# Five put-off recurrences instead of four between two expert mixtures

## The reference, cut to what matters

```python
f, i, o = sigmoid(...)   # of gates = xn @ W.T + b
z = tanh(...)
c = f * c + i * z                       # along the 512 tokens
h = o * tanh(layer_norm(c, ln_w, ln_b))
```

## Time and profile before

| | us |
|---|---|
| median of 3 runs | 1192.91 (1192.29 to 1193.06) |
| the profiled execution: its own time | 1204.18 |
| its span, first to last instruction | 1201.7 |
| last unit of the first mixture done on PE | 949.89 |
| first matmul of the second mixture | 1009.98 |

### The profile page before, as it was taken

How to read it: one execution, slowest core, us unless ns; L and a number is a source line. 1 busy time by engine, 2 the same in 40 slices (tenths; PEclk the granted TensorE clock), 3 DMA queues, 4 the chain that set the end, 5 groups by cost and what they waited for, 6 DMA issues and landing times. The chain is left out here.

```text
span 1201.7 us, 18211 instructions
## 1 busy us (share of the span) xinstructions
PE 1008.9 (84%) x5032; PEld 418.2 (35%) x5032; DVE 870.2 (72%) x1795; ACT 768.9 (64%) x1460; POOL 609.1 (51%) x632
## 2 busy tenths in 40 slices
PE   4699999999898999778998989989999874888870
PEld 3123232333333322133443443434344332454440
DVE  4698889898989898845777676767676553555554
ACT  1066666667676777666776767767777533777751
POOL 5422323332332312356678869686878630355555
PEclk9999999999999999989999999999999976999995
DMA  2462825131331402789998989896879424122126
GB/s 62 75 133 64 200 73 107 38 58 41 53 66 27 75 11 60 185 221 206 223 170 209 184 200 186 195 220 161 216 157 192 101 103 148 46 65 75 59 79 241
DMA packets 118757, 149.72 MB, mean 125 GB/s; under 512 B 18217, under 2 KB 72089, under 8 KB 118223
## 3 DMA queue, kind: packets, MB, share of 16 engines
q1 hardware_dynamic: 111854, 139.65, 50.2%
q0 software_dynamic: 6272, 8.94, 2.4%
q10 hardware_dynamic: 544, 0.13, 0.2%
HBM read 109.44 MB, written 40.04 MB: 124 GB/s over the span
## 5 line engine op out<-in xcount | busy, mean ns | idle before, releaser
L762 ACT ACTIVATE a_probs<-a_score 128x512 f32<-128x512 f32 x512 | 293.1, 597 | 126.7 <-PE a_score L843 120.1
L940 DVE TENSOR_REDUCE a_mx<-a_mxps 128x2 f32<-128x1024 f32 x256 | 306.0, 1213 | 38.1 <-PE a_mxps L834 37.5
L1539 POOL TENSOR_TENSOR m_hidl<-m_hid,m_hidh 128x512 f16<-128x512 f32 x222 | 258.0, 1176 | 98.3 <-ACT m_hidh L1602 92.7
L1811 DVE TENSOR_TENSOR m_hid<-m_h,p_gates 128x512 f32<-128x512 f32 x215 | 146.3, 686 | 73.4 <-ACT m_h L1608 53.2
L1608 ACT ACTIVATE m_h<-m_h 128x512 f32<-128x512 f32 (+1 forms) x264 | 153.5, 582 | 36.6 <-PE m_h L1716 33.7
L1602 ACT ACTIVATE m_hidh<-m_hid 128x512 f16<-128x512 f32 x222 | 137.7, 620 | 53.6 <-DVE m_hid L1811 39.1
L855 PE MATMUL a_ops<-a_probs,a_vst 128*32 128x512 f32 x1024 | 136.4, 605 | 0.8 <-ACT a_probs L762 0.8
L1694 PE MATMUL m_y<-m_hidh,p_wdh 128*128 128x512 f16 (+1 forms) x264 | 100.6, 381 | 27.6 <-POOL m_hidl L1539 25.9
L2103 POOL DMA_INDIRECT t_picked<-e_yrow,p_rows x77 | 76.1, 988 | 89.5 <-DVE e_yrow L2236 67.4
L2247 DVE SCALAR_TENSOR_TENSOR e_hidl<-e_h,e_hidh 128x468 f16<-128x468 f32 (+1 forms) x96 | 57.9, 603 | 73.9 <-ACT e_hidh L2119 45.6
L843 PE MATMUL a_score<-a_qstack,a_kstack 128*128 128x512 f16 x256 | 96.9, 384 | 8.6 <-ACT a_probs L762 7.0
(11 more groups left out here) (263 smaller groups left out, 1882.9 us busy)
## 6 DMA issues: line engine op xcount, KB each, us to landing
p_gates<-t_cw SPq DMA_DIRECT2D x256, 256.0 KB
t_slots<-p_blank SPq DMA_DIRECT2D x8, 723.9 KB
p_rows<-t_slots SPq DMA_DIRECT2D x7, 723.9 KB
t_qparts<-a_qparts SPq DMA_DIRECT2D x32, 128.0 KB
t_picked<-p_blank SPq DMA_DIRECT2D x8, 512.0 KB
p_raw<-up SPq DMA_DIRECT2D x8, 512.0 KB, 5.5
p_raw<-down SPq DMA_DIRECT2D x8, 512.0 KB, 6.3
a_xin<-x SPq DMA_DIRECT2D x8, 256.0 KB, 3.7
```

What stands on the lines that cost most here:

```text
L762: act.activation(probs[:, kt % 2, g, :], score[:, g % 2, :], ACT.Exp, scale=SCALE / (QS * QS)).then_inc(exp_done, 1)
L940: dve.tensor_reduce(mx[ahead % 2][:, j // 2, g:g + 2], mxps[:, j % 2, :, :], AX.X, ALU.max).then_inc(mx_done, 1)
L1539: pool.tensor_tensor(hidl[0:r0, k % r, :], hid[0:r0, k % r, :], hidh[0:r0, k % r, :], ALU.subtract).then_inc(lo_done[0], 1)
L1811: dve.tensor_tensor(gated, h, gates[:, q % (SLOTS * GROUP), :], ALU.mult).then_inc(mul_done, 1)
```

## The change

- Recurrence 3 leaves stage 6 and becomes the first of five put off to the gap.
- `PE_END`, `ACT_END`, `DVE_END` and `END_BANK` are new, and `POOL_END` gives POOL's order: here all eight `send` come between the `crstd` of recurrence 3 and that of 4.
- Recurrences 6 and 7 get buffers of their own (`room`): the late buffers lie in `hid`, `hidh` and `hidl`, which the units no longer need there. So 6 and 7 no longer wait for 4 and 5. The statistics exist four times.
- Semaphores that two kinds of step shared (`c_rel`) are two now (`cn_rel`, `s1_rel`); `prod_done` and `x_added` become one.
- The wait for the landing of the recurrences' stores moves from the end of the mixture's block on SP to the start of the next block, ahead of `kept_rows`.

```diff
-RECUR_IN = {1: 0, 3: 1, 5: 2, 6: 3}
-PUT_OFF = (4, 5, 6, 7)
-XN_RING = len(PUT_OFF) + 1
-DVE_END = ((7, "prod"), (4, "lin_f"), (7, "xadd"), (7, "stats"), (4, "iz"), (4, "scan"), (7, "norm"), (4, "cstats"),
-           (4, "caggr"), (7, "top0"), (7, "top1"), (5, "lin_f"), (7, "share"), (7, "slots"), (4, "cnorm"), (5, "iz"),
-           (5, "scan"), (4, "s1"), (5, "cstats"), (5, "caggr"), (6, "lin_f"), (6, "iz"), (6, "scan"), (6, "cstats"),
-           (6, "caggr"), (5, "cnorm"), (7, "lin_f"), (7, "iz"), (7, "scan"), (5, "s1"), (7, "cstats"), (7, "caggr"),
-           (6, "cnorm"), (6, "s1"), (7, "cnorm"), (7, "s1"))
+RECUR_IN = {1: 0, 3: 1, 5: 2}
+PUT_OFF = (3, 4, 5, 6, 7)
+XN_RING = len(PUT_OFF)
+PE_END = ((3, "f"), (3, "i"), (7, "prodT"), (3, "z"), (3, "o"), (4, "f"), (4, "i"), (3, "cT"), (4, "z"), (7, "xnT"),
+    (4, "o"), (7, "logits"), (3, "nT"), (5, "f"), (5, "i"), (3, "sR"), (7, "rank"), (5, "z"), (4, "cT"), (5, "o"), (6,
+    "f"), (6, "i"), (6, "z"), (6, "o"), (5, "cT"), (7, "f"), (7, "i"), (7, "z"), (7, "o"), (6, "cT"), (7, "cT"), (4,
+    "nT"), (5, "nT"), (4, "sR"), (6, "nT"), (5, "sR"), (6, "sR"), (7, "nT"), (7, "sR"))
+DVE_END = ((7, "prod"), (3, "lin_f"), (7, "xadd"), (7, "stats"), (3, "iz"), (3, "scan"), (7, "norm"), (3, "cstats"),
+    (3, "caggr"), (4, "lin_f"), (4, "iz"), (3, "cnorm"), (7, "top0"), (7, "top1"), (3, "s1"), (7, "share"), (4,
+    "scan"), (7, "slots"), (4, "cstats"), (4, "caggr"), (5, "lin_f"), (5, "iz"), (5, "scan"), (6, "lin_f"), (5,
+    "cstats"), (5, "caggr"), (6, "iz"), (6, "scan"), (7, "lin_f"), (7, "iz"), (6, "cstats"), (6, "caggr"), (7,
+    "scan"), (4, "cnorm"), (5, "cnorm"), (4, "s1"), (6, "cnorm"), (5, "s1"), (7, "cstats"), (7, "caggr"), (6, "s1"),
+    (7, "cnorm"), (7, "s1"))
+POOL_END = ((7, "rstd"), (3, "crstd"), (7, "send"), (7, "send"), (7, "send"), (7, "send"), (7, "send"), (7, "send"),
+    (7, "send"), (7, "send"), (4, "crstd"), (5, "crstd"), (6, "crstd"), (7, "crstd"))
...
     def early(self):
-        return self.index() < 2
+        return self.index() < 2 or self.index() >= BATCH - 2
+    def room(self):
+        return self.p + 2 * (self.index() >= BATCH - 2)
...
-        gate_f, cell, s1 = ([sb(f"{n}{p}", [P, TOK]) for p in range(2)] for n in ("gate_f", "cell", "s1"))
-        cn = [sb(f"cn{p}", [P, TILES, D]) for p in range(2)]
+        gate_f = buffers("gate_f", [hid[:, 4, :], hid[:, 5, :]])
+        cell, s1, cn = (buffers(n, [wide_part(t, k) for t in (hidh, hidl)]) for k, n in enumerate(("cell", "s1", "cn")))
...
             for late in PUT_OFF[1:]:
                 store_s(stage_of(late))
-            for p in range(2):
-                sp.wait_ge(s_out[p], 16 * PASSES)
...
         @block.sync
         def _(sp):
+            for p in range(2):
+                sp.wait_ge(pre.s1_out[p], 16 * PASSES)
             kept_rows(sp, scratch, kept, kept_in)
```

More of the change, by code:

```diff
@@ L143, in __init__ @@
         self.gate_in = [sem(f"gate_in{k}") for k in range(SLOTS)]
+        self.s1_out = [sem(f"s1_out{p}") for p in range(2)]
         self.blank = sb("blank", [P, REC])
@@ L1185, in bank_plan @@
             continue
[L1186 removed]
+        if key[1] in ("prodT", "xnT"):
             use(key, turn % NBANKS)
@@ L1327, in mixture_phase, with buffers, wide_part @@
         prod = sb("prod", [P, TOK])
+        def buffers(name, late):
+            return [sb(f"{name}{p}", [P, TOK])[:] for p in range(2)] + late
+        def wide_part(t, k):
+            return t[:].rearrange("p r x -> p (r x)").bitcast(F32)[:, k * TOK:k * TOK + TOK]
         xnew = sb("xnew", [P, TILES, D])
@@ L1333, in mixture_phase @@
         stats, mv = sb("stats", [P, TILES, 6]), sb("mv", [P, TILES, 2])
-        cstats, cmv = ([sb(f"{n}{p}", [P, TILES, k]) for p in range(2)] for n, k in (("cstats", 6), ("cmv", 2)))
+        cstats, cmv = ([sb(f"{n}{p}", [P, TILES, k]) for p in range(4)] for n, k in (("cstats", 6), ("cmv", 2)))
         vareps, rstd = (sb(n, [P, TILES, 1]) for n in ("vareps", "rstd"))
-        cvareps, crstd = ([sb(f"{n}{p}", [P, TILES, 1]) for p in range(2)] for n in ("cvareps", "crstd"))
+        cvareps, crstd = ([sb(f"{n}{p}", [P, TILES, 1]) for p in range(4)] for n in ("cvareps", "crstd"))
         rec = [sb(f"rec{p}", [P, TILES, REC]) for p in range(2)]
@@ L1393, in mixture_phase @@
         c_moments, c_inverse = sem("c_moments"), sem("c_inverse")
-        bias_done, s_out = sem("bias_done"), [sem(f"s_out{p}") for p in range(2)]
+        bias_done, s_out = sem("bias_done"), pre.s1_out
         top, tgap_done, shared_out, counting = (sem(n) for n in ("top", "tgap", "shares", "counting"))
@@ L1430, in bank_free @@
             else:
-                eng.wait_ge(c_rel, old.n("c_rel", 1 + (use == "nT")))
+                eng.wait_ge(cn_rel if use == "cT" else s1_rel, old.n("once", 1))
         JOB_AT = {(0, 0, 0, 8): 0, (0, 0, 0, 16): 1, (0, 0, 0, 24): 2, (0, 0, 1, 12): 3, (0, 1, 0, 12): 4,
@@ L1582, in _ @@
                 further(LAST.back(), q)
[L1583 to L1590, removed]
+            places = iter(range(SENDS))
+            for b, name in POOL_END:
+                if name == "rstd":
+                    inverse_std(stage_of(b))
+                elif name == "crstd":
+                    inverse_cell_std(stage_of(b))
+                else:
+                    send(stage_of(b), next(places))
         @block.scalar
@@ L1648, in step @@
                             else:
-                                act.wait_ge(c_rel, b.twice("c_rel", 2))
-                        act.activation(tg[name][b.p][:], src, ACT.Tanh, scale=0.5, bias=bgh[:, w:w + 1]
+                                act.wait_ge(s1_rel, b.twice("once", 1))
+                        act.activation(tg[name][b.room()], src, ACT.Tanh, scale=0.5, bias=bgh[:, w:w + 1]
                                        ).then_inc(gate_done, 1)
@@ L1657, in step @@
                     act.wait_ge(sR_full, b.n("once", 1))
-                    if not b.early():
+                    if b.index() >= 2:
                         act.wait_ge(s_out[b.p], b.half("dma", 0))
@@ L1737, in step @@
                 if name == "prodT":
-                    pe.wait_ge(prod_done, b.n("once", 1))
+                    pe.wait_ge(prod_done, b.n("sums", 1))
                     for t in range(TILES):
@@ L1844, in step @@
                     dve.tensor_tensor(bank(b, "prodT"), xres[b.p][:].rearrange("p t d -> p (t d)"), bank(b, "prodT"),
-                                      ALU.add).then_inc(x_added, 1)
+                                      ALU.add).then_inc(prod_done, 1)
                 elif name == "stats":
-                    dve.wait_ge(x_added, b.n("once", 1))
+                    dve.wait_ge(prod_done, b.n("sums", 2))
                     if not b.first():
@@ L1869, in step @@
                     dve.wait_ge(gate_done, b.n("gates_full", 1))
-                    dve.tensor_scalar(gate_f[b.p][:], bank(b, "f"), 0.5, 0.5, ALU.mult, ALU.add).then_inc(cell_step, 1)
+                    dve.tensor_scalar(gate_f[b.room()], bank(b, "f"), 0.5, 0.5, ALU.mult, ALU.add).then_inc(cell_step, 1)
                 elif name == "iz":
@@ L1874, in step @@
                     dve.wait_ge(gate_done, b.n("gates_full", 3))
-                    dve.scalar_tensor_tensor(bank(b, "z"), tg["i"][b.p][:], 1.0, bank(b, "z"), ALU.add, ALU.mult
+                    dve.scalar_tensor_tensor(bank(b, "z"), tg["i"][b.room()], 1.0, bank(b, "z"), ALU.add, ALU.mult
                                              ).then_inc(cell_step, 1)
@@ L1881, in step @@
                         dve.wait_ge(sR_full, b.twice("once", 1))
-                    dve.scalar_tensor_tensor(s1[b.p][:], tg["o"][b.p][:], 1.0, bank(b, "nT"), ALU.add, ALU.mult
-                                             ).then_inc(c_rel, 1)
+                    dve.scalar_tensor_tensor(s1[b.room()], tg["o"][b.room()], 1.0, bank(b, "nT"), ALU.add, ALU.mult
+                                             ).then_inc(s1_rel, 1)
                 elif name == "scan":
@@ L1888, in step @@
                         dve.wait_ge(cT_full, b.twice("once", 1))
-                    dve.tensor_tensor_scan(cell[b.p][:], gate_f[b.p][:], bank(b, "z"), 0.0, ALU.mult, ALU.add
+                    dve.tensor_tensor_scan(cell[b.room()], gate_f[b.room()], bank(b, "z"), 0.0, ALU.mult, ALU.add
                                            ).then_inc(cell_step, 1)
@@ L1893, in step @@
                     dve.wait_ge(cT_full, b.n("once", 1))
-                    if not b.early():
-                        dve.wait_ge(c_inverse, b.twice("inverse", 2))
+                    if b.index() >= 4:
+                        dve.wait_ge(c_inverse, b.n("inverse", 2 - 4 * PER["inverse"][0]))
                     apart(dve)
                     for t in range(TILES):
-                        dve.bn_stats(cstats[b.p][:, t, :], bank(b, "cT")[:, t * P:t * P + P]).then_inc(c_moments, 1)
```

(1 more changed line is left out.)

52 lines of the change are left out of this document (25 added, 27 removed).

## The result

The changed kernel takes 1175.61 us (median of 4 runs, 1173.87 to 1180.63), the kernel before on the same chip 1192.99 (4 runs, 1192.29 to 1193.57): ratio 0.9861, 95% interval 0.9828 to 0.9895, so 17.4 us less. The profiled execution of after has a span of 1171.2 us and an own time of 1173.87.

The account below looks back on a forecast made before the run. PE was taken to bound stage 6, and a chain across engines, laid out along DVE, the gap. Stage 4.6, gap 10.8 and moved wait 1.8 sum to 17.2 us less: 1192.9 to 1175.7, range 1171 to 1183.

Parts of the forecast that it names:

- 12.6 was forecast: Gap before the second mixture: 10.8 us less from DVE's work and holes, 1.8 from the moved wait.
- Stage 6, 4.6 less: Stage 6 without recurrence 3 becomes like stage 7: 56.0 to 51.4 us, 4.6 less; bounds 3.6 and 6.1.
- DVE's work, 38.9: In the gap, DVE's steps with hops take 32.8 us plus 6.1 for one more recurrence: 38.9.
- Holes, 5.0 taken, 4.2 laid out: DVE's waits in the new gap, 21.9 us before: layout gives 4.2, 5 taken; bounds 3 and 7.6.
- POOL is half a microsecond ahead at `cnorm` 4: In the gap after the eight sends, `crstd` 4 is ready at 980.8 and DVE reaches `cnorm` 4 at 981.3.
- PE's clock: In the gap, clock near 1.00 up to the last `o` gate, PE sparse only afterwards, when DVE leads.
- The rival of half the clock in all of the gap: PE bounds the gap at half clock: 19 us of holes, 3.2 us gained in all, 1189.7; chance 0.07.
- The moved wait, 1.8: SP's wait for store landings leaves the mixture block's end for the next block: 1.8 us less, costing nothing there.
- What could be late next: Token-row loads done at 989, next phase at 997.4, so hidden; copies of 6 and 7 waiting for stores cost 1.8 at most.
- No hole of the old size: Rival: the new order holds as many DVE holes in the gap as the old; no change, 1192.6; chance 0.04.
- No send held for a step: Rival: each POOL send in the gap is held for one DVE step of 0.69 us: 5 us lost, 1180.7; chance 0.05.
- The rule on the port pair: GpSimd transfer descriptors can't be written while a vector step holds the shared ports; 0.13 us at most in the old trace.

Follow-up runs that it names:

- experiment 10: Changed kernel with 41 matmuls whose result nobody reads added in PE's list through the end of the gap; 1171.56 us, ratio 0.9829 to the kernel before, gap 44.82.
- experiment 9: Changed kernel with the gap's `lin_f` moved from DVE to ACT and the four lists reordered, `crstd` 4 between sends; 1171.61 us, ratio 0.984, gap 43.27.
- experiment 2: Changed kernel's code (buffers, semaphores, moved wait) with the old lists and recurrence 3 back in stage 6; 1191.67 us, ratio 0.9982 to the kernel before, gap 57.60.
- run 3: Changed kernel with recurrence 3 kept in stage 6, so four recurrences in the new lists; 1181.96 us, ratio 0.9912 to the kernel before, gap 48.11.
- run 6: Also experiment 6: changed kernel with two more scans on DVE behind `caggr` 4; 1189.32 us, ratio 0.9895 to the kernel before, gap 49.46.
- second group: Four kernels on another chip: four recurrences with loads first, 1193.24 us; changed kernel with wait put back, 1186.9; with two DVE scans, 1189.32; with one POOL operation, 1185.96.

## Why the prediction came out right

The sum, 17.2 us against 17.4 measured (1175.7 against 1175.6), is right in its terms as well, but that it fits to 0.2 us is luck: errors of up to 1.4 us go against each other, and two profiles of the kernel before differ by 1.8 us in the gap that it starts from. By the table the gap gained 13.9 us between the first profiles and 12.1 between the second ones, where 12.6 was forecast.

- *Stage 6, 4.6 less.* Measured 4.8 and 5.7. The stage has 50.3 to 51.2 us, about as stage 7 had (51.4); stage 7 is 0.2 to 0.8 longer now, which the sum had at nothing.
- *DVE's work, 38.9.* Measured 42.72 from first step to last less 5.2 of waits: 37.5. The term was 1.4 too large. It was worked out from steps with waits between them. Steps without a wait between them overlap in the timeline: `lin_f` of 3 has 0.69 us, and `xadd` starts 0.60 behind its start. From start to start, waits taken out, a recurrence's seven steps are 5.7 us on average in the new gap, 5.9 in the old and 6.1 in the sum.
- *Holes, 5.0 taken, 4.2 laid out.* Measured 5.2, and at the places named: 0.45 `lin_f` (0.4), 0.35 `share` (0.4), 0.36 `s1` 4 (0.6), 0.54 `cnorm` 7 (0.7), 2.12 the last `s1` (2.1). The second profile has none before `share`, 0.77 before `s1` 4 and the same in all (5.3). Not foreseen: 0.45 before `cnorm` 4, 0.41 before `cstats` 5, 0.29 before `cnorm` 3 and 0.25 before `s1` 6. The step that failed, though not by enough to show, is that POOL is half a microsecond ahead at `cnorm` 4: it is behind by 0.45. POOL is ready 30.8 us behind the last down matmul, as laid out (30.9), and DVE already at 30.4, 1.0 sooner than the 31.4 laid out.
- *PE's clock.* The forecast was "near 1.00 up to the last `o` gate". In one profile it was 0.83 in 955 to 965 and in the other 1.00, with the same gap of 46.2; behind the last gate it is low for the last 13 to 15 us, where it costs 1.0 to 1.4 in the gap (experiment 10). The rival of half the clock in all of the gap fell.
- *The moved wait, 1.8.* `e_x` follows the last copy 1.87 sooner than it did, and with the wait put back 1.87 later again.
- *What could be late next.* The loads went out at 975.5 and were no bound. The copy of 6 waits 1.73 us for a store, as named, and ACT stands idle 0.94 us behind it before tanh 7, so it costs nothing here; in experiment 9 that air is gone.
- *The rivals.* No hole of the old size (experiment 2 shows that it was the lists that made them). No send held for a step: it is 1.28 from send to send behind the first, beside a DVE that is busy 9.32 of 10 us. The rule on the port pair that the prediction set against the change (the Trainium skill, SBUF — State Buffer, section "SBUF: two separate sides") has no cost in this trace beyond the 0.12 us of the first send. No run shows whether any of these DVE steps holds the pair.

Where I erred was in the experiments. For run 3 the layout had the lists of four engines and not SP's, and missed a store ahead of the loads: 3 us. For run 6 I had 2.05 instead of 3.2.

**The 30.5 us between the two profiles.** The extra of the first profile of before is in the second mixture, which the change doesn't touch. ACT's silu there waits 44.0 us in its 96 operations, against 33.4 in the other profile of the same kernel and 32.2 after. One of these waits, in the timelines of ACT and of PE of the kernel before:

```profile
1048.35 0.45 ACT L2138 ACTIVATE e_h<-e_h 128x351 f32<-128x351 f32 x1 [1.65 <-PE e_h L2187]
```

```profile
1046.94 0.31 PE L2187 MATMUL e_h<-e_xh,p_wul 128*128 128x351 f16 x1
```

PE is done at 1047.25 and ACT starts 1.10 us later; neither engine's rows show what it waits for. All four kernels of the second group, on the chip where the kernel before takes 1202.07, have the longer second mixture (155.8 to 160.9); none of the eight of the other two groups has it (147.0 to 149.9). So it doesn't come with the change. The first profile's own time of 1204.18 also lies among that chip's times of the kernel before (1198.95 to 1206.8) and above all 31 others (at most 1197.75), so it was probably taken on a chip like it, though no run settles that; why the silu waits longer there stays open.

## What to carry to other kernels

Where no engine is full and a chain runs through several in-order lists, lay out every list, the DMA queues' too, with measured durations: here the layout gave each hole to about 0.5 us, and the one list left out cost 3 us. An independent chain interleaved in such a stretch can be nearly free while the engine with the most steps still has holes: the fifth recurrence's 5.9 us cost 0.7. With the holes filled, work added to that engine was paid in full (2.44 us of scans, and the gap 3.2 longer), while 3.1 us taken away gave nothing until the order was made anew, and then the next bound, here a buffer that waits for its store, took its part.

## What the runs showed of the hardware

- A 256 KB store issued 2.6 us behind the last of four loads of token rows (experiment 9) landed 5.50 us after its issue (979.71 to 985.21), one issued 4.2 us behind them (the changed kernel) 3.68; the later stores of the two kernels take 2.3 to 2.6.
- PE kept at work with matmuls that nobody reads held its clock at 1.00 in a stretch that had 0.63 and 0.50, with 41 matmuls in place of idle time; behind 2.5 us of waiting in the next phase a stretch at the low level followed all the same.
- Steps of DVE that follow each other without a wait start some 0.09 us before the end of the one before: a `lin_f` of 0.69 us takes 0.60 from start to start. A `scan` that needs the `iz` before it starts 0.03 behind its end.
- Two chips differ by 0.8% on the same kernel (1192.47 and 1202.07), while DVE's steps in the gap stand at the same times on both. The silu of the second mixture waits 46.0 us in the kernel of experiment 6, on the slower one, and 32.1 in that of experiment 9, on the other; PE's rows don't account for it.
